# Flamingo block with a mixture of experts: attention and routing joined in one block, router logits from rounded halves

## What is computed

```
xn  = layernorm(x)                         # no scale, no shift
q, k, v from xn @ wq; ctx and xn @ wk, wv  # keys: 512 of the context, 512 of the rows
x2  = x + tanh(g_xattn) * (softmax(q k^T) v) @ wo
xn2 = layernorm(x2)
shared = (silu(xn2 @ W1s.T) * (xn2 @ W3s.T)) @ W2s.T      # 704 wide
probs  = softmax(xn2 @ Wg.T)                              # 16 experts
w, sel = top_k(probs, 4)
routed = sum over the 4 chosen e of w_e * (silu(xn2 @ W1[e].T) * (xn2 @ W3[e].T)) @ W2[e].T   # 352 wide
out = x2 + tanh(g_ffn) * (shared + routed)
```

## Time and profile before

| | us |
|---|---|
| median of 3 runs | 1076.47 |
| lowest, highest | 1072.86, 1079.32 |
| the profiled execution, own time | 1079.6 |
| its span | 1077.9 |
| TensorE busy | 1040.5 (97%) |
| VectorE busy | 622.9 (58%) |
| ScalarE busy | 369.6 (34%) |
| GpSimd busy | 502.6 (47%) |
| mean granted clock of TensorE | 0.98 |

### The profile page before, as it was taken

The page is one execution under the profiler, slowest core; times in us unless marked ns, Lnnn a source line. Parts: engine busy times, 40 slices in busy tenths (PEclk is TensorE's granted clock), DMA queues, the critical chain, the costliest instruction groups (busy, mean ns, idle before and its releaser), DMA issues.

```text
span 1077.9 us, 18268 instructions
## 1 busy us (share of the span) xinstructions
PE 1040.5 (97%) x5290; PEld 907.8 (84%) x5291; DVE 622.9 (58%) x1114; ACT 369.6 (34%) x673; POOL 502.6 (47%) x546
## 2 busy tenths in 40 slices
PE   5999999999999988999999999999999999999995
PEld 4888888888888867887899999999999999998884
DVE  3254356447344553889765556556555555655768
ACT  4431122113112211211354555555455455553120
POOL 5620202201120052202888787766666666654775
PEclk9999989999999996999999999999999999999998
DMA  8052455457237525522575555555555555556787
GB/s 331 23 157 105 130 195 156 156 178 236 55 121 227 188 105 221 181 77 105 166 212 173 187 169 173 176 176 172 168 182 166 171 180 165 173 175 215 225 283 258
DMA packets 80254, 186.23 MB, mean 173 GB/s; under 512 B 11552, under 2 KB 32160, under 8 KB 76960
## 3 DMA queue, kind: packets, MB, share of 16 engines
q1 hardware_dynamic: 53184, 117.26, 33.8%
q0 software_dynamic: 16672, 49.70, 15.0%
q10 hardware_dynamic: 10368, 18.88, 4.8%
HBM read 149.10 MB, written 49.28 MB: 184 GB/s over the span
## 4 chain that ended last, share of the span: by engine, by line
PE 48%; POOL 6%; DVE 3%; issue 2%; DMA 1%; ACT 0%; POOLq 0%; DVEq 0%; ACTq 0%
PE c_ps_u L89 25%; PE c_ps_y L89 14%; POOL parts L1704 6%; PE b_ps_u L89 3%; PE b_ps_y L970 2%; PE c_ps_h L1604 2%; DVE tile_hot L1240 1%; DMA parts<-y_dram,token_slots 0%; DVE b_h L1025 0%; DVE tile_hot L1245 0%; DMA y_dram<-y 0%; DVE b_h_lo L1016 0%; PE d_ps_u L89 0%; DVE slot_hot L1233 0%; DVE grid L1260 0%
## 5 line engine op out<-in xcount | busy, mean ns | idle before, releaser
L1386 POOL DMA_INDIRECT xs<-xn_dram,column x288 | 293.6, 1019 | 92.5 <-issue 89.0
L89 PE MATMUL c_ps_u<-expert_hi,xT_hi 128*128 x576 | 191.6, 333 | 0.0
L89 PE MATMUL c_ps_u<-expert_hi,xT_lo 128*128 x576 | 186.4, 324 | 0.0
L89 PE MATMUL c_ps_u<-expert_lo,xT_hi 128*128 x576 | 185.0, 321 | 0.0
L1559 DVE TENSOR_TENSOR expert_lo<-stage,expert_hi 128x1088 f32 x72 | 93.4, 1297 | 65.9 <-ACT expert_hi L1510 50.6
L89 PEld LDWEIGHTS c_ps_u<-expert_lo,xT_hi 128*128 128x128 f32 x576 | 108.9, 189 | 0.0
L89 PEld LDWEIGHTS c_ps_u<-expert_hi,xT_lo 128*128 128x128 f32 x576 | 108.4, 188 | 0.0
L89 PEld LDWEIGHTS c_ps_u<-expert_hi,xT_hi 128*128 128x128 f32 x576 | 108.2, 188 | 0.0
L1572 DVE TENSOR_TENSOR hf<-c_ps_u,gate 128x352 f32<-128x352 f32 x72 | 37.7, 524 | 110.0 <-ACT gate L1501 110.0
L1510 ACT ACTIVATE expert_hi<-stage 128x1088 f32 x72 | 80.3, 1115 | 21.1 <-issue 21.1
L89 PE MATMUL c_ps_y<-expert_hi,hT_hi 128*128 (+1 forms) x216 | 84.8, 393 | 0.7 <-DVE hT_lo L1553 0.7
(11 more groups left out here) (275 smaller groups left out, 2390.5 us busy)
## 6 DMA issues: line engine op xcount, KB each, us to landing
stage<-we SPq DMA_DIRECT2D x76, 544.0 KB, 3.7
y_dram<-y ACTq DMA_DIRECT2D x72, 256.0 KB, 2.1
xs<-xn_dram,column POOLq DMA_INDIRECT x288
ctxT_raw<-ctxT SPq DMA_DIRECT2D x4, 1024.0 KB, 6.8
ctx_raw<-ctx SPq DMA_DIRECT2D x4, 1024.0 KB, 4.8
r_t<-x SPq DMA_DIRECT2D x4, 1024.0 KB, 5.2
x_dram<-r_t SPq DMA_DIRECT2D x4, 1024.0 KB, 4.3
out<-total SPq DMA_DIRECT2D x16, 256.0 KB, 4.3
```

The lines of the kernel that those rows point to most:

```text
L89: last = pe.matmul(out, a[i], b[j], start=(n == 0), stop=(n == 3 * len(pairs) - 1))
L1386: pool.indirect_dma_start(xs[:, g, :], None, rows, bass.IndirectOffsetOnAxis(ap=sources[:, g:g + 1], axis=0)).then_inc(sem, 16)
```

## The change

- **One block.** The attention phase no longer opens its block; it returns its engine functions, and each engine runs them ahead of the routing's in the second block. GpSimd makes the routing's constants (`consts`) before the attention's last root. SyncE loads the down weights once the last rows are turned, GpSimd once a late product of attention is done.
- **Last rows.** TensorE turns the last rows ahead of pair 1 of the first half (two tiles) and amid it (two), makes their logits ahead of pair 2, turns them amid pair 2. VectorE's parts stand in `work` at 0, 1 and 2, with the ranking; ScalarE's in a `work` of its own.
- **Logits.** The router's weights are split into halves, side by side in 32 columns (`wg_both`), before the loop, where TensorE waits for them. xn2T is split (ScalarE 4 copies before `exps(0)`, VectorE 4 subtractions behind `maxima(0)`). The logits are 8 fp32r matmuls with wg_both as weights and 512 moving columns; VectorE copies the [32, 512] out, TensorE turns it back by 4 narrow transposes behind scores(2), and a sum over the two halves gives the logits. The softmax moves behind `maxima(3)`, the exponential to i == 2; scores(2) waits for the bank before its second half.
- **Leaner list.** `counts` moves from place 2 to 4, `slots` from 3 to 5, the masks' count from pair 3 to pair 5, `hot_rows` to 9 and 10, `hot_tiles` to 11 and 12. The multiplication by token numbers goes from VectorE (16 instructions) to ScalarE. The grid is replaced by one compare and one sum of 16 columns, a diagonal and one matmul with ones. LIST_AT is 15. The combine `weights` move from place 12 to the last phase's first half.

The diff, indentation left out of account and cut to its core:

```diff
-def attention_phase(nc, io, mem, keep, later, first_free, sh):
+def attention_phase(nc, c, io, mem, keep, later, first_free, sh):
...
-    wg = small("router_w", [P, 2, DC, E], F32)
+    wg_both = small("router_w_both", [P, 2, DC, 2 * E], F32R)
...
+        return lambda: sp.wait_ge(t_ready, 8 * B + 8)
...
+        consts()
             root(var2, rstd2, 2 * B)
+        pool.wait_ge(m_ready, 22 * B - 2)
...
+                for i in range(IT):
+                    o = (slice(None), slice(None), slice(i * P, (i + 1) * P))
+                    act.wait_ge(r_turned, b * 4 + (i - 3))
+                    act.activation(xn2T_hi[o], xn2T[o], ACT.Copy).then_inc(r_hi_made, 1)
...
-                    if i == 1 and b is not None:
+                if i == 2 and b is not None:
...
+        act.activation(wg_both[:, :, :, 0:E], wg[:], ACT.Copy).then_inc(wg_hi, 1)
...
-            router(B)
-        @block.vector
-        def _(dve):
+        def last_rows():
+            for i in range(IT):
+                high_t(last_xn2T_hi[:, :, i * P:(i + 1) * P])
+        return last_rows, lambda: router(B)
...
+            def logits():
+                dve.wait_ge(m_ready, m.up())
+                dve.tensor_copy((last_lgT if b is B else lgT)[:], ps_m[0:2 * E, (m.n - 1) % 2, :]).then_inc(m_free, 1)
...
-                    for k in range(2):
                         dve.wait_ge(m_ready, m.up())
-                        dve.tensor_copy(lg[:, 2 * k:2 * k + 2, :], ps_m[:, (m.n - 1) % 2, 0:2 * E].rearrange(
-                            "p (i e) -> p i e", e=E)).then_inc(m_free, 1)
+                dve.tensor_reduce(lg[:], ps_m[:, (m.n - 1) % 2, 0:2 * IT * E].rearrange("p (i h e) -> p i e h", h=2, e=E),
+                                  AX.X, ALU.add).then_inc(m_free, 1)
...
+        def split_r(b):
+            for i in range(IT):
+                o = (slice(None), slice(None), slice(i * P, (i + 1) * P))
+                dve.wait_ge(r_hi_made, b * 4 + (i - 3))
+                dve.tensor_tensor(xn2T_lo[o], xn2T[o], xn2T_hi[o], ALU.subtract).then_inc(r_split, 1)
...
+            if b is not None:
+                split_r(b)
                 maxima(1)
-                shifted()
+            logits()
                 trans(0)
                 if ahead:
                     next_sums(b)
                 maxima(2)
-                softmax()
+            shifted()
                 trans(1)
                 if ahead:
                     next_apply(b)
                 maxima(3)
+            softmax()
...
+        dve.wait_ge(wg_hi, 1)
+        dve.tensor_tensor(wg_both[:, :, :, E:2 * E], wg[:], wg_both[:, :, :, 0:E], ALU.subtract).then_inc(wg_split, 1)
...
-            for i in range(IT):
-                route_turn(i)
-            for part in route(B)[0:2]:
-                part()
+        return (last_rows, *route(B)[0:3])
...
+        def logits(w, hi, lo):
-                for k in range(2):
                     m.up()
                     pe.wait_ge(m_free, m.now - 2)
-                    for i in range(2):
+            out = ps_m[:, (m.n - 1) % 2, :]
                         for c in range(DC):
-                            last = pe.matmul(ps_m[:, (m.n - 1) % 2, i * E:(i + 1) * E],
-                                             xn2T[:, c, (2 * k + i) * P:(2 * k + i + 1) * P], wg[:, w, c, :],
-                                             start=(c == 0), stop=(c == DC - 1))
+                pe.matmul(out[0:2 * E], wg_both[:, w, c, :], hi[:, c, :], start=(c == 0), stop=False)
+            for c in range(DC):
+                last = pe.matmul(out[0:E], wg_both[:, w, c, 0:E], lo[:, c, :], start=False, stop=(c == DC - 1))
+            last.then_inc(m_ready, 1)
+        def turn_logits(lgT):
+            m.up()
+            for i in range(IT):
+                last = pe.transpose(ps_m[:, (m.n - 1) % 2, 2 * i * E:2 * (i + 1) * E], lgT[:, i * P:(i + 1) * P],
+                                    ident[0:2 * E, 0:2 * E])
...
+                if i == 2 and b is not None:
+                    pe.wait_ge(m_free, m.now)
...
-                        pe.wait_ge(r_turned, b * 4)
-                        logits(0)
+                    pe.wait_ge(r_split, b * 4)
+                    logits(0, xn2T_hi, xn2T_lo)
+                if i == 2 and b is not None:
+                    turn_logits(lgT)
...
-            pe.wait_ge(small_in, 48)
+        pe.wait_ge(wg_split, 1)
...
+        rows_turned()
         load_down(sp, later.d_raw, io, raw_in["down"])
...
+        def hot_tokens(k):
-    def vector(dve):
+            act.wait_ge(tiles_hot, k + 1)
+            act.wait_ge(const_ready, 5)
+            for j in range(HN // TOPK):
+                at, o = k * HN // TOPK + j, tile_hot[k][:, j * TOPK:(j + 1) * TOPK, :]
+                last = act.activation(o, o, ACT.Copy, scale=token[:, at:at + 1])
+            last.then_inc(hot_ready, 1)
+        work = {1: last_rows, 2: router, SC + IT + 3: lambda: hot_tokens(0), SC + IT + 4: lambda: hot_tokens(1)}
...
-            then(dve.tensor_tensor(hot[:], lane_h[:, 0:TILES_MAX].unsqueeze(1).broadcast_to([P, HN, TILES_MAX]),
+            dve.tensor_tensor(hot[:], lane_h[:, 0:TILES_MAX].unsqueeze(1).broadcast_to([P, HN, TILES_MAX]),
                                    tile_no[:, k * HN:(k + 1) * HN].unsqueeze(2).broadcast_to([P, HN, TILES_MAX]),
-                                   ALU.is_equal))
-            for j in range(HN // TOPK):
-                at = k * HN // TOPK + j
-                last = dve.tensor_scalar(hot[:, j * TOPK:(j + 1) * TOPK, :], hot[:, j * TOPK:(j + 1) * TOPK, :],
-                                         token[:, at:at + 1], None, ALU.mult)
-            last.then_inc(hot_ready, 1)
+                              ALU.is_equal).then_inc(tiles_hot, 1)
...
-            then(dve.tensor_tensor(grid[:], lane[:, 0:TILES].unsqueeze(2).broadcast_to([P, TILES, E]),
-                                   cum[:].unsqueeze(1).broadcast_to([P, TILES, E]), ALU.is_ge))
-            then(dve.tensor_reduce(t_f[:], grid[:], AX.X, ALU.add))
-            then(dve.tensor_scalar(t_f[:], t_f[:], float(E - 1), None, ALU.min))
+            then(dve.tensor_scalar(e_le[:], cum[:], token[:, 0:1], None, ALU.is_le))
+            then(dve.tensor_reduce(e_tile[:], e_le[:], AX.X, ALU.add))
+            dve.tensor_scalar(diag[:], keep["ident"][:, 0:TILES], e_tile[:, 0:1], None, ALU.mult).then_inc(hot_ready, 1)
...
-        work = {0: (rank, choices), 2: (counts,), 3: (slots,),
-                6: (lambda: hot_rows(0, piece),), 9: (lambda: hot_rows(piece, piece), lambda: hot_rows(2 * piece, piece)),
-                10: (lambda: hot_rows(3 * piece, piece), lambda: hot_tiles(0)), 11: (lambda: hot_tiles(1),),
-                12: (weights,), 13: (found_tokens, schedule), 14: (source_rows, places),
-                15: (slices, lambda: first_low(0)), 16: (lambda: experts_first(dve), lambda: first_low(1)),
-                17: (lambda: first_low(2), lambda: first_low(3))}
+        work = {0: (last_rows,), 1: (logits, shifted, softmax, larger_), 2: (equals, added, choices), 4: (counts,), 5: (slots,),
+                9: (lambda: hot_rows(0, piece), lambda: hot_rows(piece, piece)),
+                10: (lambda: hot_rows(2 * piece, piece), lambda: hot_rows(3 * piece, piece)),
+                11: (lambda: hot_tiles(0),), 12: (lambda: hot_tiles(1),), 13: (schedule,),
+                14: (found_tokens,), 15: (source_rows, places, slices, lambda: first_low(0)),
+                16: (lambda: experts_first(dve), lambda: first_low(1)), 17: (lambda: first_low(2), lambda: first_low(3))}
...
+        def ahead(n, k):
-            if n * (SC + IT) + j == LIST_AT:
+            at = n * (SC + IT) + k
+            if at == 1:
+                turn_r(0), turn_r(1)
+            if at == 2:
+                last_logits()
+            if at == SC - 1:
+                count_masks()
+            if at == LIST_AT:
                 list_slots()
-            if n * (SC + IT) + j == LIST_AT + 1:
+            if at == LIST_AT + 1:
                 turn_sources()
-            if (n, j) != (0, 3):
-                return
-            pe.wait_ge(const_ready, 6)
+        def amid(n, j):
+            if (n, j) == (0, 1):
+                turn_r(2), turn_r(3)
+            if (n, j) == (0, 2):
+                turn_logits()
...
-            pe.wait_ge(hot_ready, PIECES + 2)
+            pe.wait_ge(hot_ready, PIECES + 3)
...
+            last = pe.matmul(sh.ps_t[:, 0, 1, 0:TILES], ones[:], diag[:], start=True, stop=True)
...
+            if (n, k) == (0, 1):
+                weights()
...
-        attention_phase(nc, io, mem, keep, later, keep["end"], first)
+        attention = attention_phase(nc, c, io, mem, keep, later, keep["end"], first)
...
+            routing[0](sp, attention[0](sp))
...
+            attention[1](pool, lambda: routing[5](pool))
...
-            routing[4](pe)
+            routing[4](pe, *attention[4](pe))
```

1036 lines of the change are left out of this document (531 added, 505 removed).

## The result

The changed kernel takes 1065.94 us in the median (1064.16 to 1068.17, 4 runs), the kernel before 1076.65 (4 runs). The ratio is 0.9903 with a 95% interval of 0.9883 to 0.9923: faster by 1.0%, clear of the 0.5% that the prediction names as the least difference a measurement tells. Forecast were 1060 us and a range of 1052 to 1069, so the sign and the range held, and the gain came out at two thirds of the 16.6 us forecast. The profiled execution has a span of 1066.5 us against 1077.9, 11.4 us less.

A forecast was written before the change was run, and what follows sets the result against it. The prediction took TensorE, busy nearly all the span, as the bound, with a GpSimd gather chain at the end. Its terms sum to -16.6 us: 1063.0 from the profiled 1079.6, 1059.9 from the median; forecast 1060, range 1052 to 1069.

The forecast's parts named there:

- wait for the router weights: Before the batch loop: TensorE idles 2.0 us for wg_split, plus 0.9 for half a possible clock fall.
- logits of three batches: Score stages: wide logit matmuls at full clock replace narrow ones, gaining 4.5 + 2.9 + 2.9 = 10.3 us.
- softmax behind the fourth maximum: Batches: softmax delays k_lo(0), which frees a bank for the third wv product; 0.65 us wait per batch, +1.9 us.
- join: Between attention and routing: the 18.3 us gap and 2.0 of clock go, added TensorE work stays; net -16.3 us.
- slots before the sum: First shared half: slots delay the sum that frees ps_y; TensorE waits 3.9 us plus 1.7 of clock, +5.6.
- second half: Second shared half up to the first expert product: gain 0.7 us only, as the gather delays a sum; bounds -3 and +2.
- behind it: Last half: combine weights take 4 us of VectorE before the first combine, delaying a buffer GpSimd asks for; +0.3 us.
- Rival (d): TensorE's stream, cut at 17 places by narrow work or short waits, draws clock falls of 1.7 us each; 1085 us, chance 0.02.
- rival (a): Batches: the clock still falls since transposes and turn stay; +6.7 us, 1066.6, chance 0.12.
- (c): Shared half: weights of the shared down products land late and TensorE waits 10 us; 1070 us, chance 0.04.
- (e): The rest, above all a join gap that partly stays because up weights or batch 0 rows are late; some 1068 us, chance 0.03.
- down(2) does not wait: First shared half: VectorE is quicker than assumed, so TensorE has no wait on the sum; -5.6 us, 1054.3, chance 0.13.

The follow-up runs named there:

- e7: Changed kernel plus 16 narrow fp32 matmuls (the old amount) before the new logits in each score stage; 1082.48 us, ratio 1.0048 to the kernel before.
- e8: Changed kernel with last rows' turns and logits before the first shared product, softmax before the first h; 1174.61 us, kernel before 1228.39 on that chip.
- e1: Changed kernel with slots moved from place 5 to 7 of the first shared half; 1063.27 us, ratio 0.9866 to the kernel before.
- e2: Changed kernel with TensorE waiting for the split router weights at first use, not before the loop; 1062.26 us, ratio 0.9854 to the kernel before.
- e5: Changed kernel with VectorE taking the first gathered rows at place 17, not 16; 1063.60 us, ratio 0.9866 to the kernel before.
- e0: Changed kernel once more, unaltered; 1068.98 us, ratio 0.9907 to the kernel before.
- e4: Changed kernel with GpSimd's routing constants behind the last root, not before it; 1065.86 us, ratio 0.9887 to the kernel before.
- e10: Changed kernel with softmax moved in front of the fourth row maximum; 1154.02 us, kernel before 1233.34 on that chip.
- e3: Changed kernel with softmax and first ranking step moved behind the first k_lo; 1070.98 us, ratio 0.9942 to the kernel before.
- e6: Changed kernel plus 32 narrow fp32 matmuls (double the old amount) before the new logits in each score stage; 1100.70 us, ratio 1.0212 to the kernel before.
- e11: Changed kernel with router-weights wait at use, softmax before fourth maximum, slots in three pieces, gathered rows at 17; 1149.81 us, kernel before 1233.34 on that chip.
- e9: Changed kernel with slots at 7, router-weights wait at use, softmax behind k_lo, constants behind root, gathered rows at 17; 1150.02 us, kernel before 1228.39 there.

## Why the prediction was right, and where it was short

By its own steps, forecast against measured in the two profiled executions:

| step | forecast | measured | from |
|---|---|---|---|
| start, up to the first turn | 0 | +0.8 | 51.60, 52.36 |
| wait for the router weights | +2.9 | +4.1 | 2.3 of wait, 1.8 of clock |
| logits of three batches | -10.3 | -10.1 | 13.10, 11.47, 11.48 against 8.66 three times |
| softmax behind the fourth maximum | +1.9 | +2.5 | 15.41 us from second to fourth turn; 16.32, 16.32, 16.09 |
| rest of the batches | 0 | +1.5 | waits on pT_lo 0.47, r_t 1.10 |
| join | -16.3 | -15.7 | 51.0 us to the first output tile; 35.3 |
| slots before the sum | +5.6 | +6.2 | 15.6 us of output tiles; 21.7 |
| second half | -0.7 | -1.4 | 54.1; 52.7 |
| behind it | +0.3 | +0.7 | 557.9; 558.6 |
| sum | -16.6 | -11.4 | |

**The mechanisms were right.** Each gain and each new wait stood where the prediction had put it, and e7, e8, e1, e2 and e5 show each by its own edit: the logits' gain is work and clock together, the join's is cover for two thirds (10.6 of 15.7 us), the two waits of 3.55 and 2.10 us cost what they last and half clock behind them. What the prediction calls 32 narrow matmuls are 16, each with two records; its prices, taken by the stretch, don't change by it. The split of the logits' gain was a little off: the old 3.64 us less 1.85 for the eight and 0.36 for the turn is 1.4 us of work a batch, 4.3 in all, not 3.6, and 5.8 of clock, which e7 gives back as 5.9.

**The sum was short by 5.2 us.** Eight of the nine rows came out dearer, by 5.9 us together, and the second half cheaper by 0.7. Of the terms that the prediction had sized, the wait for the router weights missed by most, 1.2 us. The prediction took a wait of 2.0 and, of the clock, "I take half of it, +0.9"; the profile drew the fall in full (1.8 us), and the wait is 2.1 to 3.2 us, longer where GpSimd holds VectorE up. The Trainium skill's sentence that the gate looks at recent activity in a frame which runs on by itself ("TensorE: Matmul & The Clock Gate", section "What's actually happening"), by which this term is 0 or 1.7 us from run to run, is borne out in this, that the same wait had half clock behind it in some executions and not in others: behind this wait the clock fell in seven of the ten profiles that have it (e0, e1, e4, e5, e8, e10 and the first one) and not in e3, e6 and e7; behind the wait of 3.5 us on the sum it fell in nine of ten and not in e3; and it fell behind none of the twelve waits of 1.1 to 1.7 us in otherwise unbroken work. The size is not borne out: where it fell before the loop, it cost 1.5 to 1.7 us in four profiles and 2.9 to 3.1 in three (in e0 the granted clock is 0.68 from 80.75 to 90.00 us). The mean over all ten is 1.6 us, so the 0.9 of the prediction was low.

The next term is not one that was sized wrong but one that was left out: waits on pT_lo and r_t. The prediction said of the split of xn2T "I take 0" and of GpSimd's constants that they "lie in its idle time before the root"; VectorE's longer queue and, in some executions, the constants cost 1.5 us together, and how much of it is whose was not separated. Softmax, slots and join came out about 0.6 us dearer each; start and end took 1.2 us, of which nothing here says more. In the second half the wait was 1.66 us and not 2.4, and the 1.0 us taken for the clock did not come; why only 0.7 of these 1.7 us shows in the row is open.

Rival (d), a clock that falls at 17 places, had the Trainium skill's section "A second HAM failure mode: psum-queue depth-cycling", on the same page, on its side. The trace shows half clock at two places, and 1.00 in the three score stages, where TensorE's stream is cut by transposes and waits of 0.5 us. By these rows cuts of that length don't bring it; rival (a) falls with it, and e7 shows what it would have taken. Rivals (c) and (e) are out too: no wait stands in front of the first output tile, the wait in front of the third went with the slots (e1), and the first shared product starts 0.23 us behind attention's last matmul.

**The range** held with 3 us to spare on the slow side, in part by luck: in the call of e0 the same kernel took 1068.98 us, 0.02 below the upper end. Its low end took in a case (down(2) does not wait) that did not come; e1 and e11 show that it needs another place for the slots.

## What to carry to other kernels

When work is moved under a neighbour, list what stands in front of it and behind it on the engine that is moved past, and look for the first idle stretch ahead of the old place: softmax cost 2.5 us behind the fourth maximum, brought waits of 7.3 us behind the first k_lo, and cost nothing in front of the maximum. In these profiles a wait of 1.9 to 3.6 us on TensorE cost its own length and, in 21 of 30 cases up to the first expert product (waits within the join left out), 1.5 to 3.1 us of clock behind it, so a semaphore is waited for where the data is first used; and a routine in front of a sum that frees a buffer is cut in pieces before it is moved. When a barrier goes, most of the gain (10.6 of 15.7 us here) is independent work of the bound engine placed over the chain that stood at it.

## What the runs showed of the hardware

- A subtraction of 128 columns on VectorE with both inputs in SBUF took 0.28 to 1.39 us in thirteen profiles, by where GpSimd's run of subtractions (4.99 us for four) stood when it began; in all thirteen it ended 0.14 to 0.16 us behind the end of one of them. The scaling of 4 columns by the gates took 0.23 us where none of GpSimd's subtractions was under way (e3, e9) and 1.46 to 2.01 in eleven profiles beside it. The Trainium skill, "SBUF — State Buffer", section "SBUF: two separate sides", says that the two engines share a pair of ports that one of them holds for a whole instruction; these rows agree for the subtraction; the scaling went on over GpSimd's constants in four of the eleven (the first profile, e5, e6, e10).
- Half clock came in the midst of unbroken work: during or just behind the 16 matmuls of 16 columns (3.64 us in the third batch) in all three stages of e7, but not behind 8 transposes of 128 columns with wide matmuls around them.
- An fp32 matmul of 16 columns leaves two records in the profile (e7 adds 3 x 16 of them and 96 records: 5307 against 5211), an fp32 transpose one, so a count of records is not a count of instructions.
